# Last group of a three-layer interaction network: three chunks per tile scaled in PSUM by ScalarE, the last tile combined on VectorE, three output row blocks turned inside the group

## The reference

```python
for W, b in params:
    z = jnp.einsum('bhd,bfd->bhfd', x_vec, input)       # h: rows of the layer's input, f: 64 fields
    z = z.reshape(B, h * f, d)
    x_vec = jnp.einsum('oc,bcd->bod', W, z) + b[None, :, None]
    outs.append(x_vec.sum(axis=2))
return jnp.concatenate(outs, axis=1)                    # 512 x 384
```

## Time and profile before

| | us |
|---|---|
| median of 3 runs | 1128.33 |
| range of the runs | 1128.06 to 1129.62 |
| profiled execution | 1127.95 |
| its span (first to last instruction) | 1126.2 |
| PE busy in the span | 1095.7 (97%) |
| DVE busy | 868.8 (77%) |
| ACT busy | 451.4 (40%) |
| POOL busy | 836.8 (74%) |

### The profile page before, as it was taken

One profiled execution on the slowest core, in us unless ns is written; L12 is line 12 of the kernel. 1 busy time (PEld: TensorE's weight loads), 2 busy tenths in 40 slices (PEclk: granted clock), 3 DMA queues, 4 the chain that ended last, 5 costly groups with the idle time before them and its releaser, 6 DMA issues.

```text
span 1126.2 us, 17047 instructions
## 1 busy us (share of the span) xinstructions
PE 1095.7 (97%) x4690; PEld 786.3 (70%) x4690; DVE 868.8 (77%) x3008; ACT 451.4 (40%) x1533; POOL 836.8 (74%) x765
## 2 busy tenths in 40 slices
PE   5989999999999999999999999999999999999996
PEld 5766667666677667666678666676677776666776
DVE  3556879888884888879794798978887598888990
ACT  1443435343432444434351343534343243434550
POOL 4568887969784697878875788787978479697561
PEclk9999999999999999999999999999999999999998
DMA  7952414223141231405141051423323142240000
GB/s 245 251 114 60 112 54 94 73 56 104 17 122 36 58 102 24 124 27 122 46 103 47 17 122 45 105 62 80 87 42 95 31 94 73 51 109 9 1 1 29
DMA packets 112352, 85.82 MB, mean 76 GB/s; under 512 B 75136, under 2 KB 77920, under 8 KB 112128
## 3 DMA queue, kind: packets, MB, share of 16 engines
q1 hardware_dynamic: 110528, 78.37, 28.9%
q10 hardware_dynamic: 1728, 6.36, 1.5%
HBM read 14.75 MB, written 0.79 MB: 14 GB/s over the span
## 4 chain that ended last, share of the span: by engine, by line
PE 83%; DVE 13%; issue 2%; DMA 1%; ACT 1%; POOL 1%; SPq 0%; POOLq 0%; ACTq 0%
PE y L692 53%; PE l L705 19%; DVE acc L619 8%; PE xt L755 5%; PE l2p L767 3%; DVE bd L584 2%; DVE w1l L673 1%; DVE x1l L594 1%; DMA gram<-in_L_rec_W_dram 1%; PE l2p L744 1%; DMA z<-xg 0%; PE l2p L717 0%; ACT prod L525 0%; PE xt L737 0%; PE l L727 0%
## 5 line engine op out<-in xcount | busy, mean ns | idle before, releaser
L619 DVE SCALAR_TENSOR_TENSOR acc<-y,x0t,acc 128x128 f32<-128x128 f32 x2560 | 698.8, 341 | 206.1 <-PE y L692 204.0
L525 ACT ACTIVATE prod<-y,x0t 128x128 f32<-128x128 f32 x1280 | 366.0, 369 | 610.5 <-PE y L692 578.7
L692 PE MATMUL y<-w1h,x1h 128*128 128x512 f32 x1024 | 509.3, 497 | 6.0 <-DVE acc L619 4.3
L692 PE MATMUL y<-w1h,x1l 128*128 128x512 f32 x1024 | 403.5, 394 | 0.0
L692 PE MATMUL y<-w1l,x1h 128*128 128x512 f32 x1024 | 402.4, 393 | 0.0
L371 POOL TENSOR_TENSOR pacc<-pacc,prod 128x512 f32<-128x512 f32 x192 | 247.4, 1289 | 191.6 <-ACT prod L525 191.6
L360 POOL TENSOR_TENSOR z<-z,xg 128x512 f32<-128x512 f32 (+2 forms) x272 | 348.3, 1288 | 23.7 <-DMA z<-xg 23.7
L692 PEld LDWEIGHTS y<-w1h,x1h 128*128 128x128 f32 x1024 | 192.8, 188 | 132.8 <-issue 59.2
L705 PE MATMUL l<-z,w0t 128*128 128x512 f32 (+1 forms) x512 | 257.5, 585 | 0.6 <-POOL z L360 0.6
L692 PEld LDWEIGHTS y<-w1l,x1h 128*128 128x128 f32 x1024 | 192.8, 188 | 82.2 <-issue 54.1
L692 PEld LDWEIGHTS y<-w1h,x1l 128*128 128x128 f32 x1024 | 192.1, 188 | 43.6
(11 more groups left out here) (65 smaller groups left out, 300.8 us busy)
## 6 DMA issues: line engine op xcount, KB each, us to landing
z<-xg SPq DMA_DIRECT2D x480, 128.0 KB, 2.4
xg<-in_r_input_dram SPq DMA_DIRECT2D x32, 128.0 KB, 3.9
w2t<-in_L_rec_W_dram ACTq DMA_DIRECT2D x8, 512.0 KB, 7.1
gram<-in_L_rec_W_dram SPq DMA_DIRECT2D x8, 512.0 KB, 5.9
z<-xg SPq DMA_DIRECT2D x32, 96.0 KB, 4.0
z<-xg SPq DMA_DIRECT2D x15, 192.0 KB
gram<-in_L_rec_W_dram ACTq DMA_DIRECT2D x1, 2048.0 KB, 7.9
out_dram<-z SPq DMA_DIRECT2D x4, 192.0 KB, 2.1
```

The source lines that it names most:

```text
L525: last = nc.scalar.activation(prod[:, h % HSLOTS, k, :], y[c % YB][:, k * O:(k + 1) * O], ACT.Copy, scale=x0t[:, j, f:f + 1])
L619: ins = nc.vector.scalar_tensor_tensor(out=to, in0=of, scalar=x0t[:, j, f:f + 1], in1=b1r[:] if m == 0 else to, op0=ALU.mult, op1=ALU.add)
L692: ins = nc.tensor.matmul(to, stationary, moving, start=(first and k == 0), stop=(last and k == 2))
```

## The change

- In the last group chunks 3, 9 and 12 of each tile go another way. ACT scales them where they lie in PSUM (four activations), and DVE adds the whole bank in one instruction of 128 x 512 instead of four of 128 x 128. That instruction waits for ACT and for the end of DVE's chunk before; the chunk behind it waits for its end.
- The last tile is combined by DVE, one addition and one reduction over the four slices, instead of POOL's three additions.
- The layer-0 bias is added at e = 6 of the last group.
- Blocks 0, 1 and 2 of the output are turned at e = 34, 40 and 46 of the last group (all in its third tile) into `l0`, copied by ACT and stored. Only block 3 is left for the end, copied by ACT.

```diff
+SCALED = ()
+SCALED_LAST = (3, 9, 12)
+LAST_TILES = (GROUPS - 1) * TILES
+ROWS_AT = (34, 40, 46)
...
             for r in range(B // P):
-                sp.wait_ge(outs_made[r % 2], r // 2 + 1)
+                sp.wait_ge(outs_made, r + 1)
                 sp.dma_start(out[r * P:(r + 1) * P, :], outs[:, r, :]).then_inc(stored, 16)
...
             groups(pool, body)
-            combine(GROUPS * TILES - 1, 1)
...
+            def row_out(r):
+                act.wait_ge(turned, r + 1)
+                nc.scalar.copy(outs[:, r, :], l0[:, 0:L * O]).then_inc(outs_made, 1)
...
                     if c in HELPED:
                         multiply(tile, j, c)
+                    elif c in scaled_in(tile):
+                        scale(tile, j, c)
...
+                    if kind == "last" and e in ROWS_AT:
+                        row_out(ROWS_AT.index(e))
...
+            def scale(tile, j, c):
+                act.wait_ge(y_made, CHUNKS * tile + c + 1)
+                for k in range(CF):
+                    f = CF * c + k
+                    of = y[c % YB][:, k * O:(k + 1) * O]
+                    last = nc.scalar.activation(of, of, ACT.Copy, scale=x0t[:, j, f:f + 1])
+                last.then_inc(y_scaled, 1)
...
             quarter_out(QUARTERS)
-            for r in range(0, B // P, 2):
-                act.wait_ge(turned, r + 1)
-                nc.scalar.copy(outs[:, r, :], y[r][:, 0:L * O]).then_inc(outs_made[0], 1)
+            row_out(B // P - 1)
...
+                if c in scaled_in(tile):
+                    dve.wait_ge(y_scaled, scaled_at(tile, c))
+                    dve.wait_ge(acc_step, added(tile, SUMMED[m - 1]))
+                    to = acc[:, j % 2].rearrange("p k o -> p (k o)")
+                    nc.vector.tensor_tensor(to, y[c % YB][:], to, ALU.add).then_inc(acc_step, 1)
+                    return
                 dve.wait_ge(y_made, CHUNKS * tile + c + 1)
+                after_scaled = m > 0 and SUMMED[m - 1] in scaled_in(tile)
...
+                    if after_scaled and k == 0:
+                        dve.wait_ge(acc_step, added(tile, SUMMED[m - 1]))
+                    elif m > 0 and not after_scaled and k % 2 == 0:
+                        dve.wait_ge(acc_step, added(tile, SUMMED[m - 1]) + (k + 2 - CF))
...
+                    if e == SUM_AT and kind == "last":
+                        dve.wait_ge(l0_used, GROUPS)
+                        nc.vector.tensor_scalar(sums0, sums0, b0d[:, 0:1], None, ALU.add).then_inc(sums_made, 1)
...
             groups(dve, body)
-            dve.wait_ge(l0_used, GROUPS)
-            nc.vector.tensor_scalar(sums0, sums0, b0d[:, 0:1], None, ALU.add).then_inc(sums_made, 1)
-            for r in range(1, B // P, 2):
-                dve.wait_ge(turned, r + 1)
-                nc.vector.tensor_copy(outs[:, r, :], y[r][:, 0:L * O]).then_inc(outs_made[1], 1)
+            tile, slot = GROUPS * TILES - 1, 1
+            dve.wait_ge(pool_step, pool_at(tile, HN - 1))
+            dve.wait_ge(acc_step, tile_added(tile))
+            nc.vector.tensor_tensor(acc[:, slot], acc[:, slot], pacc[:], ALU.add).then_inc(acc_step, 1)
+            dve.wait_ge(acc_step, tile_added(tile) + 1)
+            dve.wait_ge(l2p_made, layer2_ready(tile - 2))
+            nc.vector.tensor_reduce(x2[:, slot], acc[:, slot].rearrange("p k o -> p o k"), AX.X,
+                                    ALU.add).then_inc(x2_made, 1)
...
+            def turn_row(r):
+                pe.wait_ge(sums_made, 1)
+                pe.wait_ge(l2_used, r + 2)
+                if r > 0:
+                    pe.wait_ge(outs_made, r)
+                for k in range(L):
+                    last = nc.tensor.transpose(l0[:, k * O:(k + 1) * O], sums[:, k, r * P:(r + 1) * P], ident[:])
+                last.then_inc(turned, 1)
...
                     chunk(tile, j, c)
+                    if kind == "last" and e in ROWS_AT:
+                        turn_row(ROWS_AT.index(e))
...
-            pe.wait_ge(sums_made, 1)
-            pe.wait_ge(l2_used, QUARTERS + 1)
-            for r in range(B // P):
-                for k in range(L):
-                    last = nc.tensor.transpose(y[r][:, k * O:(k + 1) * O], sums[:, k, r * P:(r + 1) * P], ident[:])
-                last.then_inc(turned, 1)
+            turn_row(B // P - 1)
```

More of the change, by code:

```diff
@@ L47 @@
 SUMMED = tuple(c for c in range(CHUNKS) if c not in HELPED)
-SN = CF * len(SUMMED)
+SCALED = ()
+SCALED_LAST = (3, 9, 12)
+LAST_TILES = (GROUPS - 1) * TILES
 HSLOTS = 3
@@ L191, in cin_kernel @@
         prod_made = sem("prod_made")
+        y_scaled = sem("y_scaled")
         pool_step = sem("pool_step")
@@ L199, in cin_kernel @@
         turned = sem("turned")
-        outs_made = [sem("outs_made0"), sem("outs_made1")]
+        outs_made = sem("outs_made")
         stored = sem("stored")
@@ L232, in z_rows, with in_last, scaled_in, add_steps @@
             return P if t < ZT - 1 else ZCOPIES * ZLAST
-        def tile_added(tile):
-            return SN * tile + 2 * SN
+        def in_last(tile):
+            return isinstance(tile, int) and tile >= LAST_TILES
+        def scaled_in(tile):
+            return SCALED_LAST if in_last(tile) else SCALED
+        def add_steps(scaled, upto):
+            return sum(1 if c in scaled else CF for c in SUMMED if c <= upto)
+        SN = add_steps(SCALED, CHUNKS)
+        def added_before(tile):
+            if in_last(tile):
+                return SN * LAST_TILES + SN + add_steps(SCALED_LAST, CHUNKS) * (tile - LAST_TILES)
+            return SN * tile + SN
+        def added(tile, c):
+            return added_before(tile) + add_steps(scaled_in(tile), c)
+        def tile_added(tile):
+            return added_before(tile + 1)
+        def scaled_at(tile, c):
+            before = len(SCALED) * tile
+            if in_last(tile):
+                before = len(SCALED) * LAST_TILES + len(SCALED_LAST) * (tile - LAST_TILES)
+            return before + scaled_in(tile).index(c) + 1
         def x2_ready(tile):
@@ L612, in add_fields @@
                     to, of = acc[:, j % 2, k, :], y[c % YB][:, k * O:(k + 1) * O]
-                    if m > 0 and k % 2 == 0:
-                        dve.wait_ge(acc_step, SN * tile + (SN + CF * (m - 1) + k + 2))
+                    if after_scaled and k == 0:
+                        dve.wait_ge(acc_step, added(tile, SUMMED[m - 1]))
+                    elif m > 0 and not after_scaled and k % 2 == 0:
+                        dve.wait_ge(acc_step, added(tile, SUMMED[m - 1]) + (k + 2 - CF))
                     if m == 0 and k > 0:
@@ L777, in chunk @@
                 else:
-                    value = SN * tile + (SN + CF * SUMMED.index(before) + CF) - (SN if late else 0)
-                    pe.wait_ge(acc_step, value)
+                    pe.wait_ge(acc_step, added(tile - 1 if late else tile, before))
                 cols = slice(j * P, (j + 1) * P)
```

## The result

The changed kernel takes 1125.71 us (median of 18 runs, 1125.15 to 1127.87), the kernel before 1128.18 in the same rounds. The medians lie 2.47 us apart. The ratio of the two kernels' runs is 0.9981, 95% interval 0.9974 to 0.9988, or about 2.1 us: a small gain, clear of noise, that falls on the edge of the 0.2% which the prediction took as its measure (the median is under its 1126.07, the ratio is not quite under 0.998). One of the 18 runs of the kernel before took 2519.59 us; the other 17 lie between 1126.62 and 1129.62, and the median doesn't feel it. The profiled execution took 1125.61 us, its span is 1123.9.

What follows compares the result with a forecast made beforehand. DVE was taken to bound the last group, PE 0.2 us a tile behind, then one serial chain. Terms -0.4 + 0.53 + 1.14 - 1.4 - 2.8 - 1.06 = -4.0 gave 1124.3 us, range 1123.3 to 1127.6.

Steps and rivals of the forecast that it cites:

- rival A: PE's clock falls all the same in the pause before the last layer2: 1127.1 us or between, chance 0.33.
- The group as a whole: Last group: scaled chunks -0.4, bias +0.53 and turned blocks +1.14 us taken together, +1.27.
- Scaled chunks: Last group, chunks 3, 9 and 12 scaled by ACT: 0.1 us gained a tile, -0.4 in all.
- rival C: Last group: ACT's four activations on one PSUM bank don't overlap, 1.7 instead of 1.14 us; 1133.6 us, chance 0.05.
- Bias: Layer-0 bias moved from the end into the last group, where DVE is the bound: +0.53 us.
- Blocks in the group: Three output blocks turned in the last group's third tile cost PE 0.43 us each: +1.14 us.
- Combination: Last tile, DVE's last product to layer2: 1.5 us on DVE instead of 2.89, -1.4, bounds -1.6 and -1.0.
- Pause: PE's wait behind the last chunk, before the last layer2: 3.0 us instead of 4.54.
- Clock: PE's clock does not fall at a 3.0 us pause, so last layer2 and quarter run quicker: -2.8 us.
- End: After the last quarter: only one block left to turn, copy and store, -1.06 us, bounds -0.8 and -1.5.

Runs made afterwards that it cites:

- e2: Changed kernel with all four output blocks turned, copied and stored at the end and the bias added there, as before the change: 1126.87 us, ratio 0.9988.
- e1: Changed kernel with no chunk scaled by ACT, all else kept: 1126.31 us, ratio 0.9984 to the kernel before.
- e8: Changed kernel with chunk 12 alone scaled instead of 3, 9 and 12: 1125.36 us, ratio 0.9974 to the kernel before.
- e11: Changed kernel with the layer-0 bias added by ACT at e = 8 instead of DVE at e = 6: 1125.59 us, ratio 0.9982.
- e6: e4 with the last combination's reduction replaced by two additions: 1124.12 us, ratio 0.9965 to the kernel before.
- e5: The kernel before, with 17 unneeded matmuls filling PE's pause behind the last chunk: 1126.21 us, ratio 0.9980.
- e12: The changed kernel, unaltered, measured once more: 1126.49 us, ratio 0.9986 to the kernel before.
- e10: Changed kernel with 6 unneeded matmuls in PE's pause, leaving 2.07 us of it: 1126.23 us, ratio 0.9983.
- e4: Changed kernel with 12 unneeded matmuls filling PE's pause behind the last chunk: 1123.82 us, ratio 0.9966 to the kernel before.
- e7: e6 with only chunk 12 scaled, the bias on ACT at e = 8, blocks turned at e = 9, 19 and 35: 1122.75 us, ratio 0.9953.

## Why the prediction was right, and where it was wrong

The time, 1125.71, lies inside the stated range (1123.3 to 1127.6), 1.4 us above the value given, and the sign was right. It lies inside because the range was widened for rival A; it is outside the forecast's own range, 1123.4 to 1125.3, and the largest term of the sum failed. Its steps:

*The group as a whole: right by luck.* +1.27 was forecast (-0.4, +0.53, +1.14), +1.31 measured. Two errors of nearly half a microsecond cancel: scaling came out 0.5 worse than forecast (0.08 by e2), the blocks 0.4 better.

*Scaled chunks: sign wrong.* -0.4 was forecast; undoing them shortens the group by 0.28 (e1). The mechanism was the one laid out: chunks 3 and 9 wait for ACT (7 waits, 2.8 us), chunk 12 doesn't. The step that failed is the value taken between the ends, 0.1 us a tile of gain: the account for one tile came to 0 on DVE alone, and nothing in it gave a gain. Chunk 12 alone is worth -0.37 (e8), the other two cost 0.65. ACT's time was right (four in 1.12 us in PSUM, 1.14 into SBUF); rival C has no footing. The Trainium skill, page "ScalarE: Activation LUTs", section "Step-by-step: what each stage is for", says that ScalarE writes to PSUM faster than to SBUF; the trace agrees in sign, with 0.02 us for four.

*Bias: right*, 0.53 forecast, 0.51 (e11).

*Blocks in the group: the term was too large.* 1.14 was forecast; 1.23 for blocks and bias together (e2), less 0.51, leaves 0.72. Without scaled chunks it is 0.52 (e1's 52.24 less the 51.21 before and 0.51): the other 0.2 come with the scaled chunks, whose waits for ACT are longer in the third tile. A block takes 0.33 us of PE, not 0.43; I had scaled it from four transposes whose operand is strided, and whether the stride is the reason no run shows. That three blocks cost less than 3 x 0.33 I put down to PE's room, for which the prediction took off only 0.15; no run tests that.

*Combination: mis-sized.* -1.4 was forecast, -1.00 measured, the bound that had been named for a slow reduction: 1.02 us for 512 elements in, which take 0.675 when they are contiguous. e6 shows that it is the reduction, since two additions take 0.27 us less. The contiguous one also writes fewer results (32 columns, not 128), so the stride as the reason is likely but not shown.

*Pause: right by its working*, 3.0 forecast, 3.42 with the reduction 0.35 longer.

*Clock: the step that failed.* "At 3.0 I forecast that it does not fall", -2.8. It fell, and gave -1.1 in the profiled execution and -0.4 in another of the same kernel. With the clock kept up the term is -2.6 (L to Q 16.06 in e5 against 18.69), since the quarter then takes 14.56 us and not 14.4. Rival A was the truth, in the middle form that it mentioned. The reasoning was wrong too: the 4.2 us between PE's going idle and the fall in the one trace of before are no bound. The same kernel fell after 2.2 us (e12) and after 4.7 (1099.11 to 1103.8, with `layer2` between), and a pause of 2.07 us is enough (e10). With pauses of 0.75 us at most it never fell there (e4 to e7), nor after the wait of 1.5 us near the start in any of the traces. What sets the moment and whether the low stretch is 3.4 or 6.8 us stays open; it changes with nothing changed in the program.

*End: mechanism right, term too small.* -1.06 was forecast, -1.66 measured; -1.11 of it are the copies, and -0.55 the last store, which no longer follows closely on three others (e2, with the four back at the end, needs 2.86 again). It is past the bound of -1.5 that I had given.

So the errors of the combination (+0.4) and of the clock (+1.7) stand against that of the end (-0.6), and leave 1.5 us.

## What to carry to other kernels

Before work is handed from a bound engine to an idle one, lay the second engine's time onto the moments at which the first would pick the data up: where the first would take it up at once, it waits (chunks 3 and 9, seven times in eight, 0.20 to 0.65 us), and where another instruction lies before (here `bd`, or layer 0's work in the first tile), it gains. Work moved out of a serial end into a bound loop is worth only what the end gets shorter by, less what the loop gets longer by (here about 1.6 less 1.2 us). When several moves are tried at once, measure each alone before crediting one: e7's group looked as if the blocks had become free, and most of its gain was the bias and the scaled chunks. A serial end of small steps in front of a matmul phase can cost the clock as well as the wait, and needless matmuls in the pause bring that back: 1.5 us in the changed kernel, 2.6 us in the kernel before, the largest single gain in this study.

## What the runs showed of the hardware

- TensorE's clock fell from 2.4 to 1.2 GHz in all ten traces whose pause before the last `layer2` was between 2.07 and 4.54 us, 2.2 to 4.7 us after the engine went idle. The pause's length doesn't order it: six pauses of 3.40 to 3.55 us (after, e1, e2, e8, e11, e12) show falls from 2.2 to 4.7 us. The low stretch was 3.4 us in the two traces in which the fall came last, 4.7 us after PE went idle and just ahead of the quarter (after, e8), and 6.8 us in the eight others. The same program shows both: L to Q 17.57 us and 18.29.
- The clock stayed at 2.4 GHz over pauses of 0.43 to 0.75 us there (e4 to e7), and over a wait of 1.52 to 1.54 us near the start in all fourteen traces. Between 1.54 and 2.07 us nothing was measured.
- A reduction on DVE over four slices 128 elements apart, 512 elements in and 128 out, took 1.02 us; over 16 neighbouring elements, 512 in and 32 out, 0.675. Two additions doing the same as the first took 0.42 and 0.29.
- Four activations of 128x128 from a PSUM bank into the same bank took 1.12 us, into SBUF 1.14.
